# Delta rule kernel: unsigned bf16 matrix, first residual as two bf16 products, Wo loaded by quads, a PSUM bank of its own for the projection of v, a new static order

## The chip, the cores and the metric

One core of a Trainium2 chip. The metric is the device time of one launch in microseconds; lower is better.

## The reference, cut to what matters

The input x is 8 batches of 256 tokens of width 256. A modulated layer norm feeds a gated delta rule attention with 32 heads (keys of 48, values of 96), and a mixture of experts follows. Only the attention is touched:

```python
q = short_conv(h @ Wq, conv_q_w); k = short_conv(h @ Wk, conv_k_w)   # each followed by silu, 4 taps
v = short_conv(h @ Wv, conv_v_w)
q, k = l2norm(q), l2norm(k)
g = -exp(A_log) * softplus(h @ Wa + dt_bias); beta = sigmoid(h @ Wb)
def step(S, inp):                     # one token
    S = S * exp(g_t)
    delta = (v_t - k_t @ S) * beta_t
    S = S + outer(k_t, delta)
    return S, (q_t * scale) @ S
o = rmsnorm(o, gnorm_w) * silu(h @ Wg)
out = o.reshape(b, t, VD) @ Wo
```

## The kernel before, in words

`delta_rule` does the attention in 64 steps: 8 quads of four heads (the outer loop), each with 8 batches. A step treats 256 tokens as two chunks (c = 0, 1) of 128 tokens. Within a chunk the recurrence is a triangular system (I + A) w = r for each head, 128 x 128. `scores` and `decayed` make A (in `am`, plane 0, f32, with the query part in plane 1). An approximate inverse `tf` is built in bf16 from small blocks (`block`, `rows`, `base`, `expand`, `narrow1`, `narrow2`, `widen`, `merge1`, `merge2`). Then `w0` applies `tf` to the right side, and two rounds (REFINE = 2) refine it: `residual(c, r)` computes (I + A) w on TensorE with f32 operands and subtracts it from the right side on VectorE, giving `r16`; `delta(c, r)` adds `tf` times `r16` into the same bank CW, and ScalarE copies the sum to `w`. Chunk 0 yields the state S (`state_out`), which `ks` applies for chunk 1. `mean`, `gated`, `oT`, `wo`, `acc` finish the output.

The bf16 copy of A, `b16`, holds minus A. ScalarE makes it in `negate` directly from `am`; then GpSimd (in the helper `select`, called at the place `negate`) sets ones on the diagonals of `b16` and of `am` by two affine selects. ScalarE does not wait for GpSimd there.

The steps are a software pipeline of four stages. A turn runs one stage of four consecutive steps. `PLAN` gives a place to every piece; `TURN` sorts it by the place modulo 15 and every engine issues its own part of each piece in that order. Engines are in-order queues joined by semaphores, so a wait holds everything behind it on the same engine. There are 67 turns, of which 64 or so carry nearly all the pieces.

The eight PSUM banks are A0, A1, X0, X1, X2, CW, CX, CO; X2 is not used. `proj(n)` makes two of the six projected tiles (n = 0 and 1: q, k and part of v; n = 2: the rest of v) in banks A0, A1, A0. ScalarE scales them into `y`, VectorE adds three taps per tile (`taps(n, part)`), and ScalarE applies silu. `scores` also writes A0 and A1, so it waits in the first chunk until all taps have read their banks. GpSimd computes the squares, the decay diagonal (`gains`), the serial 8-row inverse (`base`, 15 small instructions), `root`, `keys_gain`, `keys_scale`, `block` and the output scale (`mean`). All of Wo (3072 KB) is loaded once, before the attention.

Of the kernel before, what the change touches and what calls it, by code (L numbers as in the profile page):

```python
# [63 lines left out]
PLAN = ((2.794, ("proj", 0)), (3.109, ("taps", 0, 0)), (3.26, ("taps", 0, 1)), (4.413, ("proj", 1)),  # L64
        (5.17, ("taps", 1, 0)), (5.463, ("silu", 0)), (5.907, ("taps", 1, 1)), (6.765, ("silu", 1)),
        (7.002, ("taps", 2, 0)), (7.474, ("gains",)), (7.927, ("proj", 2)), (8.48, ("norms",)),
        (9.634, ("taps", 2, 1)), (10.227, ("keys",)), (10.613, ("decays", 0)), (10.759, ("scores", 0)),
        (11.281, ("decayed", 0, 0)), (11.32, ("decayed", 0, 1)), (11.382, ("silu", 2)), (12.837, ("negate", 0)),
        (13.74, ("decays", 1)), (13.969, ("keys_scale",)), (14.149, ("decayed", 1, 0)), (14.381, ("scores", 1)),
        (14.667, ("decayed", 1, 1)), (14.991, ("negate", 1)), (16.191, ("gate", 0)), (17.05, ("gate", 1)),  # L70
        (17.595, ("root",)), (19.98, ("keys_gain",)), (20.599, ("values", 0)), (21.157, ("block",)),
        (21.281, ("round", 0)), (21.957, ("values", 1)), (24.173, ("rows",)), (26.886, ("base",)),
# [3 lines left out]
        (39.65, ("residual", 0, 0)), (40.95, ("delta", 0, 0)), (43.39, ("residual", 0, 1)),  # L76
        (43.577, ("delta", 0, 1)), (44.661, ("state_out",)), (45.952, ("ks",)), (46.296, ("w0", 1)),
        (46.395, ("mean", 0)), (47.508, ("gated", 0)), (47.55, ("residual", 1, 0)), (47.909, ("delta", 1, 0)),
        (49.242, ("oT", 0)), (49.665, ("residual", 1, 1)), (49.751, ("acc", 0)), (50.348, ("wo", 0)),
        (50.476, ("delta", 1, 1)), (50.81, ("out", 1)), (51.613, ("mean", 1)), (52.656, ("gated", 1)),  # L80
        (56.151, ("oT", 1)), (58.509, ("wo", 1)), (59.018, ("acc", 1)))
# [371 lines left out]
def delta_rule(nc, A, mem, scr):  # L453

    with ExitStack() as ctx:
# [169 lines left out]
        def _(pe):  # L625
            on = {n: nothing for n in PIECES}

            def merge1(st, l):
# [84 lines left out]
            def norms(st):  # L713
# [3 lines left out]
                for c in range(CH):  # L717
                    at = T + c * 2 * QH
                    for t in range(KTL):
                        last = pe.matmul(ps[:, A1, at:at + 2 * QH], sq[:, t, c * P:(c + 1) * P],  # L720
                                         const[:, C_HEAD + t * 2 * QH:C_HEAD + (t + 1) * 2 * QH],
                                         start=(t == 0), stop=(t == KTL - 1))
# [1000 lines left out]
```

## Time and profile before

| | |
|---|---|
| median of 3 runs | 2382.16 us (2377.2 to 2392.59) |
| the profiled execution | 2376.38 us; span 2374.4 us |
| TensorE busy | 2167.4 us, 91% |
| VectorE busy | 1801.3 us, 76% |
| GpSimd busy | 1420.4 us, 60% |
| ScalarE busy | 1196.1 us, 50% |
| the attention's turns | about 75 to 2035 us of the span |

The shares mix three phases: preparation (until 75 us), the attention, and the experts (from about 2035 us). The change is read from the middle phase, where the turns repeat. A matmul record's length contains the pipeline's latency, so the cost of a group to TensorE is the distance from its start to the next group's start.

### The profile page before, as it was taken

The numbers are of one execution on the slowest core, as the hardware profiler recorded it, in microseconds if no ns is written. First come the engines' busy times: TensorE is split into PE (matmuls) and PEld (weight loads), VectorE is DVE, ScalarE is ACT, GpSimd is POOL, SyncE is SP. The second block draws the span as 40 slices with busy tenths as digits, with TensorE's granted clock in tenths as the row PEclk, the third lists the DMA queues.
The fourth block names the chain that finished last, engine by engine and source line by source line (L and its number), as shares of the span: only waits on it lengthen the run. The fifth ranks groups of instructions, "written<-read, shape, count | busy, mean of one in ns | idle before, by whom it ended". The sixth has DMA issues, their size and how long they took to land. (4 is left out here: it accounts for less than half of the span.)

```text
span 2374.4 us, 50717 instructions
## 1 busy us (share of the span) xinstructions
PE 2167.4 (91%) x17776; PEld 1721.6 (73%) x17776; DVE 1801.3 (76%) x3955; ACT 1196.1 (50%) x3011; POOL 1420.4 (60%) x2176
## 2 busy tenths in 40 slices
PE   6489999999999999999999999999999998799997
PEld 2367777777777777777777777777777776455665
DVE  5678888888888888888888888888888885145544
ACT  4245555555555555555555555555555554222221
POOL 2567777777777777777777777777777774000000
PEclk9789999999999999999999999999999997799998
DMA  4211221112111211222112212212121110401100
GB/s 134 64 35 37 39 61 35 36 39 59 36 40 36 59 39 37 39 57 39 39 36 59 39 36 39 60 36 39 36 59 37 39 28 2 135 1 36 36 10 9
DMA packets 203838, 102.82 MB, mean 43 GB/s; under 512 B 97010, under 2 KB 185147, under 8 KB 203587
## 3 DMA queue, kind: packets, MB, share of 16 engines
q1 hardware_dynamic: 203266, 99.46, 18.5%
q8 instruction: 144, 2.36, 0.4%
q14 instruction: 108, 0.88, 0.1%
q10 hardware_dynamic: 320, 0.13, 0.0%
HBM read 69.69 MB, written 2.54 MB: 30 GB/s over the span
## 5 line engine op out<-in xcount | busy, mean ns | idle before, releaser
L911 DVE SCALAR_TENSOR_TENSOR dr_y<-dr_ps,cw,dr_y 128x255 f32<-128x255 f32 (+2 forms) x1152 | 476.1, 473 | 137.2 <-ACT dr_y L1044 137.2
L772 PE MATMUL dr_ps<-dr_w,dr_am 128*128 128x96 f32 x3072 | 438.0, 288 | 22.4 <-ACT dr_w L1096 22.4
L772 PEld LDWEIGHTS dr_ps<-dr_w,dr_am 128*128 128x128 f32 x3072 | 396.2, 198 | 57.5 <-ACT dr_w L1096 46.7
L1096 ACT COPY dr_w<-dr_ps 128x384 f32<-128x384 f32 x384 | 184.3, 480 | 292.0 <-PE dr_ps L772 292.0
L1044 ACT ACTIVATE dr_y<-dr_ps,cw 128x256 f32<-128x256 f32 x384 | 160.9, 470 | 138.8 <-PE dr_ps L704 137.2
L1194 POOL TENSOR_TENSOR dr_fo<-dr_vo,dr_nhalf 128x4 f32<-128x4 f32 x128 | 129.5, 1012 | 149.7 <-DVE dr_vo L982 145.0
L704 PE MATMUL dr_ps<-hT,wqk 128*128 128x256 f32 x768 | 195.5, 392 | 20.8 <-PEq L145 20.8
L955 DVE TENSOR_TENSOR dr_am<-dr_ps,dr_dec 128x512 f32<-128x512 f32 x256 | 164.9, 686 | 61.5 <-PE dr_ps L755 59.8
L1160 POOL TENSOR_TENSOR dr_dg<-const,dr_gam 128x512 f32<-128x512 f32 x128 | 130.3, 1039 | 126.5 <-DVE dr_gam L947 126.5
L838 PE MATMUL dr_ps<-wo,dr_oT 128*128 128x256 f32 x768 | 199.2, 397 | 1.1 <-ACT dr_oT L1132 1.0
L755 PE MATMUL dr_ps<-dr_qk 64*128 64x256 f32 x1024 | 161.2, 437 | 42.1 <-DVE dr_y L911 29.1
L733 PE MATMUL dr_ps<-wg,hT 128*128 128x384 f32 x512 | 194.8, 504 | 1.9 <-DVE dr_am L955 1.9
L704 PE MATMUL dr_ps<-hT,wv 128*128 128x256 f32 x768 | 186.9, 379 | 1.2 <-DVE dr_y L911 1.2
L1152 POOL TENSOR_TENSOR dr_sq<-dr_sy 128x256 f32<-128x256 f32 x128 | 75.7, 612 | 184.4 <-ACT dr_sy L1058 184.4
L1217 POOL TENSOR_TENSOR dr_xt<-dr_xb,dr_ab 128x56 f32<-128x56 f32 (+6 forms) x448 | 154.5, 345 | 39.4 <-ACT dr_ab L1092 0.2
L969 DVE TENSOR_TENSOR dr_r<-dr_rhs,dr_ps 128x384 bf16<-128x384 f32 x256 | 139.8, 546 | 49.5 <-PE dr_ps L772 49.5
L704 PEld LDWEIGHTS dr_ps<-hT,wqk 128*128 128x128 f32 x768 | 138.0, 193 | 36.0 <-issue 21.7
L923 DVE TENSOR_TENSOR_SCAN dr_dec<-dr_abc,dr_dg 128x512 f32<-128x512 f32 x128 | 160.8, 1256 | 0.1
L838 PEld LDWEIGHTS dr_ps<-wo,dr_oT 128*128 128x128 f32 x768 | 143.4, 201 | 16.5 <-ACT dr_oT L1132 1.5
L704 PEld LDWEIGHTS dr_ps<-hT,wv 128*128 128x128 f32 x768 | 140.9, 190 | 18.1 <-DVE dr_y L911 1.6
L755 PEld LDWEIGHTS dr_ps<-dr_qk 64*128 64x128 f32 x1024 | 98.2, 204 | 72.2 <-DVE dr_y L911 53.5
L1220 POOL TENSOR_TENSOR dr_xb<-dr_xb,dr_xt 128x56 f32<-128x56 f32 (+6 forms) x448 | 124.5, 278 | 35.1
(219 smaller groups left out, 4814.9 us busy)
## 6 DMA issues: line engine op xcount, KB each, us to landing
dr_abc<-scr_a SPq DMA_DIRECT2D x64, 512.0 KB, 5.4
dr_qk<-dr_sy SPq DMA_DIRECT2D x384, 48.0 KB, 2.0
dr_bcb<-scr_b SPq DMA_DIRECT2D x128, 64.0 KB, 4.8
dr_c<-dr_b SPq DMA_DIRECT2D x512, 4.0 KB, 1.8
dr_qk<-dr_sy SPq DMA_DIRECT2D x128, 32.0 KB, 1.9
ex_modb<-scr_mod SPq DMA_DIRECT2D x4, 1024.0 KB, 8.0
wv<-in_Wv SPq DMA_DIRECT2D x8, 384.0 KB, 3.5
wo<-in_Wo SPq DMA_DIRECT2D x1, 3072.0 KB, 12.0
```

The costliest lines, as they stand in the source:

```text
L704: last = pe.matmul(ps[:, BANK[n], j * T:(j + 1) * T], wt, hT[:, k, (it % B) * T:(it % B + 1) * T], start=(k == 0), stop=(k == KT - 1))
L733: last = pe.matmul(ps[:, (A0, A1)[c], 0:QV], hT[:, k, at:at + P], wg[:, k, :], start=(k == 0), stop=(k == KT - 1))
L755: last = pe.matmul(ps[:, (A0, A1)[side], a * 2 * P:(a + 1) * 2 * P], qk[lo:lo + 64, a, c, 0, :], qk[lo:lo + 64, a, c, :, :].rearrange("p n ...
L772: last = pe.matmul(ps[:, bank, h * DV:(h + 1) * DV], wt(h), x[:, h * DV:(h + 1) * DV], start=(start and h == 0), stop=(h == QH - 1), skip_ ...
L838: last = pe.matmul(ps[:, CO, 0:D], oT[:, t, :], wo[:, (it // B) * VT + t, :], start=(t == 0), stop=(t == VT - 1))
L911: v.scalar_tensor_tensor(y[:, slot, x:T], ps[:, BANK[n], off:off + T - x], cw[:, t, TAPS - 1 - x:TAPS - x], y[:, slot, x:T], ALU.mult, ALU ...
L923: v.tensor_tensor_scan(flat(dec[:, us, :]), flat(abc[:, m, c]), flat(dg[:, us, :]), 0.0, ALU.mult, ALU.add).then_inc(s["dec_ok"], 1)
L955: v.tensor_tensor(out, ps[:, (A0, A1)[side], :].rearrange("p (a n t) -> p a n t", a=PAIRS, n=2), bc(tri, 2, 2), ALU.mult).then_inc(s["am_o ...
L969: v.tensor_tensor(r16[:], rhs[:, m, c], ps[:, CX, 0:QV], ALU.subtract).then_inc(s["rs_ok"], 1)
L1044: act.activation(y[:, t % 4, :], ps[:, BANK[n], j * T:(j + 1) * T], ACT.Copy, scale=cw[:, t, TAPS - 1:TAPS]).then_inc(s["tap0"], 1)
L1096: act.copy(w[:, c, :], ps[:, CW, 0:QV]).then_inc(s["w_ok"], 1)
L1217: pool.tensor_tensor(xt[:, :, 0:left], bc(xb[:, :, j], 2, left), ab[:, j, :, j + 1:BASE], ALU.mult).then_inc(s["xs"], 1)
```

## The change: what it does

1. `b16` (minus A) becomes `a16` (plus A). The order of the two engines is turned: GpSimd first sets the diagonal of `am` (a piece of its own, `select`), then ScalarE casts it to `a16` (`negate`, now a plain copy waiting for GpSimd's `ia_ok`). The second affine select goes. The signs move into constants (masks) and into scales of ScalarE's copies.
2. The first residual of each chunk (r = 0) uses bf16: GpSimd makes `lo16` = am - a16 (piece `low`), and TensorE computes `a16` x `x16` plus `lo16` x `x16`, eight bf16 matmuls in place of four f32 ones. `x16` is minus the first solution, rounded to bf16 by ScalarE in `w0`; VectorE's `residual` adds instead of subtracting.
3. `delta(c, 0)` begins with one bf16 matmul of 384 columns by a negative identity `idn`, which restarts the sum in bank CW.
4. `proj(2)` writes the bank X2. `scores(0)` no longer waits for all taps but for those of `proj(0)`; `norms` is cut into two pieces, one per chunk.
5. Wo is loaded in parts of 384 KB, one per quad, into two alternating buffers.
6. `PLAN` has new places. On TensorE the order was: gate 0, narrow1 0, narrow2 0, w0 1, gate 1, narrow1 1, residual 1 0, narrow2 1, proj 0, delta 1 0, merge1 0, oT 0, proj 1, residual 1 1, wo 0, delta 1 1, merge2 0, values 0, out 1, merge1 1, values 1, proj 2, merge2 1, norms, w0 0, rows, residual 0 0, keys, scores 0, delta 0 0, oT 1, residual 0 1, wo 1, delta 0 1, scores 1, state_out, ks. It is now: ks, gate 0, gate 1, narrow1 0, w0 1, narrow2 0, residual 1 0, proj 0, narrow1 1, delta 1 0, oT 0, narrow2 1, proj 1, residual 1 1, merge1 0, wo 0, delta 1 1, values 0, merge2 0, out 1, merge1 1, values 1, proj 2, norms 0, merge2 1, norms 1, w0 0, rows, residual 0 0, keys, delta 0 0, oT 1, scores 0, residual 0 1, wo 1, delta 0 1, scores 1, state_out. On VectorE, `widen 1` now comes after `taps 0`, and `expand` after `ks`. On ScalarE `negate` 0 and 1 both follow the copies of `state_out` and precede that of `ks`; the gate's silus precede the copy of `w0 1`. On GpSimd, `select` 0 and 1 follow `base`, and `low`, `keys_gain`, the squares, `root`, `low`, `keys_scale`, `block` follow `mean 0`.

```diff
-PLAN = ((2.794, ("proj", 0)), (3.109, ("taps", 0, 0)), (3.26, ("taps", 0, 1)), (4.413, ("proj", 1)),
...
+PLAN = ((3.346, ("proj", 0)), (3.934, ("taps", 0, 0)), (4.167, ("taps", 0, 1)), (4.259, ("silu", 0)),
+        (5.544, ("proj", 1)), (7.832, ("taps", 1, 0)), (9.099, ("taps", 1, 1)), (9.319, ("silu", 1)),
+        (10.403, ("proj", 2)), (10.405, ("norms", 0)), (10.646, ("taps", 2, 0)), (10.696, ("gains",)),
+        (11.131, ("norms", 1)), (11.458, ("keys",)), (11.671, ("decays", 0)), (11.718, ("taps", 2, 1)),
+        (11.882, ("silu", 2)), (12.12, ("decayed", 0, 0)), (12.196, ("scores", 0)), (12.354, ("decayed", 0, 1)),
+        (13.634, ("decays", 1)), (13.825, ("scores", 1)), (13.831, ("select", 0)), (14.066, ("decayed", 1, 0)),
+        (14.166, ("select", 1)), (14.243, ("negate", 0)), (14.323, ("negate", 1)), (14.908, ("decayed", 1, 1)),
+        (15.869, ("gate", 0)), (16.014, ("gate", 1)), (16.781, ("low", 0)), (17.949, ("keys_gain",)),
+        (22.374, ("root",)), (22.752, ("values", 0)), (23.124, ("low", 1)), (23.185, ("keys_scale",)),
+        (23.656, ("block",)), (24.594, ("values", 1)), (25.169, ("round", 0)), (26.267, ("rows",)),
+        (27.391, ("base",)), (31.191, ("expand",)), (31.525, ("narrow1", 0)), (32.093, ("narrow2", 0)),
+        (32.93, ("widen", 0)), (33.497, ("narrow1", 1)), (34.109, ("narrow2", 1)), (34.998, ("widen", 1)),
+        (36.455, ("merge1", 0)), (38.215, ("merge2", 0)), (39.446, ("merge1", 1)), (40.621, ("merge2", 1)),
+        (41.188, ("w0", 0)), (41.444, ("residual", 0, 0)), (41.722, ("delta", 0, 0)), (42.317, ("residual", 0, 1)),
+        (42.66, ("delta", 0, 1)), (44.222, ("state_out",)), (45.358, ("mean", 0)), (45.459, ("ks",)),
+        (46.802, ("w0", 1)), (47.679, ("gated", 0)), (47.689, ("residual", 1, 0)), (48.602, ("delta", 1, 0)),
+        (48.824, ("oT", 0)), (51.162, ("residual", 1, 1)), (51.505, ("acc", 0)), (51.802, ("wo", 0)),
+        (51.903, ("delta", 1, 1)), (53.861, ("out", 1)), (55.155, ("mean", 1)), (56.485, ("gated", 1)),
+        (56.762, ("oT", 1)), (57.553, ("wo", 1)), (58.124, ("acc", 1)))
...
-        BANK = (A0, A1, A0)
+        BANK = (A0, A1, X2)
...
+            def out_weights(q):
+                wait(sp, s["wo_ps"], (q - 1) * B * CH)
+                sp.dma_start(wo[:, q % 2], A["Wo"][q * QV:(q + 1) * QV, :].rearrange("(t p) n -> p t n", p=P)
+                             ).then_inc(s["wo_ld"], 16)
...
                 if n == 2:
-                    pe.wait_ge(s["tap"], it * NT * 3 + 6)
+                    wait(pe, s["tap"], it * NT * 3)
...
-                        pe.wait_ge(*((s["tap"], (it + 1) * NT * 3), (s["kc_ok"], it + 1))[side])
+                        pe.wait_ge(*((s["tap"], it * NT * 3 + 6), (s["kc_ok"], it + 1))[side])
...
-                pe.wait_ge(s["ia_ok"], it * CH + c + 1)
-                heads(CX, lambda h: am[:, m, c * QH + h, 0, :], w[:, c, :], True).then_inc(s["res_ps"], 1)
+                if r == 0:
+                    pe.wait_ge(s["lo_ok"], it * CH + c + 1)
+                    heads(CX, lambda h: a16[:, m, c * QH + h, :], x16[:, c, :], True)
+                    heads(CX, lambda h: lo16[:, m, c * QH + h, :], x16[:, c, :], False).then_inc(s["res_ps"], 1)
+                else:
+                    pe.wait_ge(s["ia_ok"], it * CH + c + 1)
+                    heads(CX, lambda h: am[:, m, c * QH + h, 0, :], w[:, c, :], True).then_inc(s["res_ps"], 1)
...
+                if r == 0:
+                    pe.matmul(ps[:, CW, 0:QV], idn[:], x16[:, c, :], start=True, stop=False, skip_group_check=True)
...
-                act.wait_ge(s["am_ok"], it * 4 + 2 * c + 2)
-                act.activation(b16[:, m, c * QH:(c + 1) * QH, :], am[:, m, c * QH:(c + 1) * QH, 0, :], ACT.Copy,
-                               scale=-1.0).then_inc(s["b16_c"], 1)
+                act.wait_ge(s["ia_ok"], it * CH + c + 1)
+                act.copy(a16[:, m, c * QH:(c + 1) * QH, :], am[:, m, c * QH:(c + 1) * QH, 0, :]).then_inc(s["a16_ok"], 1)
...
-                copy_w(it, c, 0)
+                act.activation(x16[:, c, :], ps[:, CW, 0:QV], ACT.Copy, scale=-1.0).then_inc(s["w_ok"], 1)
...
-                wait(pool, s["b16_c"], it * CH + c + 1)
-                pool.affine_select(b16[:, m, us, :], b16[:, m, us, :], [[0, QH], [-1, P]], ALU.not_equal, 1.0, base=0,
-                                   channel_multiplier=1).then_inc(s["b16_ok"], 1)
+                pool.wait_ge(s["am_ok"], it * 4 + 2 * c + 2)
                 pool.affine_select(am[:, m, us, 0, :], am[:, m, us, 0, :], [[0, QH], [-1, P]], ALU.not_equal, 1.0, base=0,
                                    channel_multiplier=1).then_inc(s["ia_ok"], 1)
+
+            def low(st, c):
+                it, m = st
+                us = slice(c * QH, (c + 1) * QH)
+                pool.wait_ge(s["a16_ok"], it * CH + c + 1)
+                pool.tensor_tensor(lo16[:, m, us, :], am[:, m, us, 0, :], a16[:, m, us, :], ALU.subtract).then_inc(s["lo_ok"], 1)
```

## Rows read from the trace of the kernel before

**Rows 1.** Windows view, one turn: length; busy PE, PEld, DVE, ACT, POOL; granted clock; DMA.
```profile
840.00:869.20 29.20, 27.48 (x262) 23.12 (x264) 25.22 (x54) 17.03 (x44) 21.63 (x34) 1.00 0.19 39
```

**Rows 2.** Timeline of TensorE in that turn: start us, length us, line, result<-operands, records.
```profile
843.33 0.35 PE L677 MATMUL dr_ps<-dr_c32t,dr_b 128*128 128x32 bf16 x8
844.20 0.36 PE L688 MATMUL dr_ps<-dr_w,dr_tt 128*128 128x32 bf16 x8 [0.52 <-DVE dr_w L884]
844.50 0.33 PE L772 MATMUL dr_ps<-dr_rhs,dr_tf 128*128 128x96 bf16 x4
844.67 1.52 PE L733 MATMUL dr_ps<-wg,hT 128*128 128x384 f32 x4
...
846.23 1.11 PE L772 MATMUL dr_ps<-dr_w,dr_am 128*128 128x96 f32 x8
847.18 0.35 PE L688 MATMUL dr_ps<-dr_w,dr_tt 128*128 128x32 bf16 x8
847.38 1.97 PE L704 MATMUL dr_ps<-hT,wqk 128*128 128x256 f32 x8
...
861.53 1.13 PE L772 MATMUL dr_ps<-dr_w,dr_am 128*128 128x96 f32 x8 [0.16 <-ACT dr_w L1096]
862.50 0.38 PE L742 MATMUL dr_ps<-const,dr_qk 128*128 128x128 f32 x2
863.51 1.14 PE L755 MATMUL dr_ps<-dr_qk 64*128 64x256 f32 x8 [0.63 <-DVE dr_y L911]
...
872.53 0.35 PE L677 MATMUL dr_ps<-dr_c32t,dr_b 128*128 128x32 bf16 x8
```

**Rows 3.** Waits of TensorE, 500 to 1800 us (44 turns): total us, times, longest.
```profile
PE dr_ps L688 <- DVE dr_w L884: 22.9, 44, 0.5
```

**Rows 4.** Waits of VectorE in the same stretch, same columns.
```profile
DVE acc L994 <- PE dr_ps L838: 13.9, 43, 0.3
```

**Rows 5.** Timeline of VectorE in the same turn.
```profile
848.06 0.55 DVE L863 TENSOR_TENSOR dr_tn<-dr_c32t,bd 128x768 bf16<-128x768 bf16 x1
...
850.26 2.43 DVE L911 SCALAR_TENSOR_TENSOR dr_y<-dr_ps,cw,dr_y 128x255 f32<-128x255 f32 x6 [0.34 <-ACT dr_y L1044]
...
856.05 1.25 DVE L911 SCALAR_TENSOR_TENSOR dr_y<-dr_ps,cw,dr_y 128x254 f32<-128x254 f32 x3
...
867.13 1.27 DVE L923 TENSOR_TENSOR_SCAN dr_dec<-dr_abc,dr_dg 128x512 f32<-128x512 f32 x1
```

**Rows 6.** Timeline of ScalarE in the same turn.
```profile
841.94 0.62 ACT L1080 ACTIVATE dr_b<-dr_am 128x512 bf16<-128x512 f32 x1
...
857.11 0.58 ACT L1014 CAST dr_w<-dr_ps 64x512 bf16<-64x512 f32 x1
857.72 0.51 ACT L1086 CAST dr_rhs<-dr_rhs 128x384 bf16<-128x384 f32 x1
...
858.45 0.40 ACT L1060 ACTIVATE dr_vT<-dr_y 128x256 f32<-128x256 f32 x1
...
859.18 0.84 ACT L1044 ACTIVATE dr_y<-dr_ps,cw 128x256 f32<-128x256 f32 x2
```

**Rows 7.** Page, costliest groups: the copy of w.
```profile
L1096 ACT COPY dr_w<-dr_ps 128x384 f32<-128x384 f32 x384 | 184.3, 480 | 292.0 <-PE dr_ps L772 292.0
```

**Rows 8.** Timeline of GpSimd in the same turn.
```profile
861.91 2.04 POOL L1160 TENSOR_TENSOR dr_dg<-const,dr_gam 128x512 f32<-128x512 f32 x2 [1.90 <-DVE dr_gam L947]
863.89 1.20 POOL L1212 COPY dr_xb<-const 128x64 f32<-128x64 f32 x1
...
867.40 1.05 POOL L1217 TENSOR_TENSOR dr_xt<-dr_xb,dr_ab 128x32 f32<-128x32 f32 x1
868.53 0.25 POOL L1220 TENSOR_TENSOR dr_xb<-dr_xb,dr_xt 128x32 f32<-128x32 f32 x1
...
870.58 0.64 POOL L1180 TENSOR_SCALAR_AFFINE_SELECT dr_b<-dr_b 128x512 bf16<-128x512 bf16 x1
871.17 0.82 POOL L1182 TENSOR_SCALAR_AFFINE_SELECT dr_am<-dr_am 128x512 f32<-128x512 f32 x1
```

More of the change, by code:

```diff
@@ L62 @@
 ATANH = [1.0 / (2 * k + 1) for k in range(9)]
-PLAN = ((2.794, ("proj", 0)), (3.109, ("taps", 0, 0)), (3.26, ("taps", 0, 1)), (4.413, ("proj", 1)),
[L65 to L72, printed above, removed]
[3 rows of a table removed]
[L76 to L81, printed above, removed]
@@ L491, in delta_rule @@
         r16 = sb("r16", [P, QV], BF16)
+        x16 = sb("x16", [P, CH, QV], BF16)
+        lo16 = sb("lo16", [P, NB, U, P], BF16)
+        idn = sb("idn", [P, P], BF16)
         S = sb("S", [P, PAIRS, 2 * DV])
@@ L557, in delta_rule @@
         PIECES = ("merge1", "merge2", "w0", "delta", "residual", "ks", "out", "state_out", "mean", "gated", "oT", "wo",
-                  "acc", "rows", "block", "base", "expand", "narrow1", "narrow2", "widen", "proj", "silu", "taps", "gate", "norms", "gains", "root", "keys_gain", "decays", "keys", "keys_scale", "scores", "decayed", "negate",
+                  "acc", "rows", "block", "base", "expand", "narrow1", "narrow2", "widen", "proj", "silu", "taps", "gate", "norms", "gains", "root", "keys_gain", "decays", "keys", "keys_scale", "scores", "decayed", "select", "negate", "low",
                   "values", "round")
@@ L606, in blocks @@
                     rows = slice(2 * BASE * n, 2 * BASE * (n + 1))
-                    sp.dma_start(c16[rows], b16[rows, m, :, rows]).then_inc(s["c_st"], 16)
+                    sp.dma_start(c16[rows], a16[rows, m, :, rows]).then_inc(s["c_st"], 16)
             gate_weights(0)
@@ L635, in merge1 @@
                 for u in range(U):
-                    last = pe.matmul(ps[:, X0, u * 2 * HALF:(u + 1) * 2 * HALF], b16[:, m, u, :], cols[:, u],
+                    last = pe.matmul(ps[:, X0, u * 2 * HALF:(u + 1) * 2 * HALF], a16[:, m, u, :], cols[:, u],
                                      start=True, stop=True)
@@ L716, in norms @@
                 pe.wait_ge(s["sq_ok"], (it + 1) * KTL)
[L717 to L722, printed above, removed]
+                at = T + c * 2 * QH
+                for t in range(KTL):
+                    last = pe.matmul(ps[:, A1, at:at + 2 * QH], sq[:, t, c * P:(c + 1) * P],
+                                     const[:, C_HEAD + t * 2 * QH:C_HEAD + (t + 1) * 2 * QH],
+                                     start=(t == 0), stop=(t == KTL - 1))
                 last.then_inc(s["n_ps"], 1)
@@ L836, in wo_ @@
                 pe.wait_ge(s["oT_ok"], (it * CH + c + 1) * VT)
+                if c == 0:
+                    wait(pe, s["wo_ld"], it // B * 16)
                 for t in range(VT):
-                    last = pe.matmul(ps[:, CO, 0:D], oT[:, t, :], wo[:, (it // B) * VT + t, :],
+                    last = pe.matmul(ps[:, CO, 0:D], oT[:, t, :], wo[:, it // B % 2, t, :],
                                      start=(t == 0), stop=(t == VT - 1))
@@ L1221, in base @@
                     ins.then_inc(s["xb_ok"] if j == BASE - 2 else s["xs"], 1)
-            on.update(keys_scale=keys_scale, base=base, block=block, silu=squares, gains=gains, root=root, keys_gain=keys_gain, negate=select, mean=scale)
+            on.update(keys_scale=keys_scale, base=base, block=block, silu=squares, gains=gains, root=root, keys_gain=keys_gain, select=select, low=low, mean=scale)
             pool.memset(qk[:], 0.0).then_inc(s["set_ok"], 1)
```

48 lines of the change are left out of this document (26 added, 22 removed), and 3 rows, old and new, of the table PLAN.

## The prediction

> **What bounds the kernel now.** I read the totals first: TensorE is the busiest engine, but a share over three phases says little. So I went to the turns of the attention. Most of them repeat to a few hundredths of a microsecond. One instance, `narrow1 0` to `narrow1 0`, is 843.33 to 872.53, a period of 29.20 us [rows 2]. In a window of that length TensorE is busy 27.48 us and VectorE 25.22; GpSimd has 21.63 and ScalarE 17.03; the clock is 1.00, the upper level of 2.4 GHz [rows 1]. Two engines are nearly full, so the turn is set by TensorE's work plus those waits that VectorE, ScalarE and GpSimd cause it. The waits can be read as distances from start to start. `narrow1 0` holds the engine 0.87 us although its work is some 0.20 (`narrow2 1`, which does not wait, takes 847.18 to 847.38), because `narrow2 0` needs VectorE's masked copy: 0.52 us in each of 44 turns [rows 3]. `keys` takes 862.50 to 863.51, the last 0.63 of it waiting for the last tap [rows 2].
>
> **Part 1, the two bf16 products.** An f32 set of four head matmuls costs TensorE 0.97 us (861.53 to 862.50) or 0.95 (846.23 to 847.18); the bf16 set of the same shape 0.17 (844.50 to 844.67) [rows 2]. So `residual(c, 0)` falls from 0.96 to 2 x 0.17 = 0.34, twice a turn: 1.24 us less. `delta(c, 0)` gains one bf16 matmul of 384 columns, the same columns as the set: 0.17, twice, 0.34 more (bounds 0.10, without the three other weight loads, and 0.38, if an f32-like latency showed). Net 0.90 us less work per turn.
>
> The f32 set costs 5.6 times the bf16 set here [rows 2]. The Trainium skill (FP8 and Floating Point Precision, TensorE Precision Notes) says that true f32 makes four passes through the array; by that rule two bf16 products would cost half an f32 set, 0.48, and the net gain would be 0.62 us a turn. The rows' price is the one I use in the sum.
>
> **Part 2, waits on TensorE.** `w0 1` now stands between `narrow1 0` and `narrow2 0`, so the 0.52 us wait [rows 3] shrinks by 0.17 to about 0.35. The wait for the last tap in `scores(0)` goes, but `scores` had another lower bound just behind: `keys` ends at 862.88 and ScalarE's copy of about 0.4 has to follow, so that alone would free about 0.2 of the 0.63. The new order puts `delta 0 0` and `oT 1` there instead, which hides it, while `delta 0 0` itself may wait for VectorE. Together with the 0.90 us, TensorE could gain up to 1.5 us if nothing else were late. That is the floor, not the forecast.
>
> **Part 3, VectorE.** Its instructions are the same in number and form; only the order changes. In the order of after, `widen 1`, the taps of `proj 0` and `proj 1`, and what lies between form one dense block. Before, the block from `widen 1` to the last tap of `proj 1` ran from 848.06 to 857.30, 9.24 us, of which it stood 0.34 for ScalarE's copy and 0.32 (13.9/44) for `wo` [rows 4, 5]: 8.58 of work. The taps now come first, so that `widen 1` delays `residual 1 1`, `merge1 0` and all behind.
>
> **Part 4, GpSimd and ScalarE.** Out goes one affine select per chunk (0.64), in comes one subtraction of 128x512. The trace has no such instruction; `dg` of the same size takes 2.04 for two, 1.02 each, and the select 0.64 [rows 8]; between these I take 1.02, since it also has two operands. Net 0.4 x 2 = 0.8 us more (0 to 1.0), on an engine with 7.6 us idle, with its result needed only most of a turn later: nothing on the path. What is on the path is the new order of hands. Before, ScalarE cast A at 841.94 without asking GpSimd [rows 6]. Now the cast waits for `select`, and `select` stands behind `base`, which ends at 870.58, some 7 us after it starts [rows 8]. Behind the cast, on ScalarE, queue the rounding of chunk 1's right side (`ks`), the two gate silus and the copy `x16`; for `x16` TensorE's `residual 1 0` waits, and behind that `proj 0` with the next step's whole front.
>
> **The chain that sets the turn.** From the start of `proj 0` to the start of the next, with hops of about 0.05: `proj 0` 1.97 + 0.05 [rows 2]; ScalarE's two copies 0.84 + 0.03 [rows 6]; VectorE's block 8.58; then on ScalarE the last silu and the square (858.45 to 859.18) 0.73, the `merge1 1` copy (857.11 to 857.72) 0.61, `round` about 0.41 (its 0.51 less overlap), `proj 2` copies 0.84, hop 0.05: 2.64 [rows 6]; from their end (860.02) to the start of `dg` (861.91), which is three taps and `gains`: 1.89 [rows 6, 8]; `dg` 1.98 and `base` 6.69 (863.89 to 870.58) [rows 8]; two selects 1.25; the second cast 0.62 + 0.05; the rounding 0.51 + 0.05; two gate silus of 0.38 from start to start (an estimate from the 0.48 copy of the same size less 0.1 of overlap) 0.76; the `x16` copy 0.48 + 0.05 [rows 7]; `residual 1 0` 0.34. The sum is 2.02 + 0.87 + 8.58 + 2.64 + 1.89 + 8.67 + 1.25 + 0.67 + 0.56 + 1.63 = 28.78 us. The parallel leg without GpSimd, from `gains` over `decays`, taps, `decayed`, `scores 1`, `ks` and both gates to `proj 0`, I walked in the same way at about 28.3. The longer one sets the turn: 28.7 to 28.8 instead of 29.20. TensorE's 0.90 us then mostly turns into waiting.
>
> **Edits costed at nothing.** X2 for `proj 2`: its old wait (the first taps) is long satisfied before it starts. Wo by quads: seven transfers of 384 KB during the attention, issued behind those for the gate and ahead of `blocks`, whose data is wanted half a turn later; the wait in front of them asks for an output eight steps old. The smaller first load shortens nothing that waits. The split `norms`, `idn` and the new constants: the same records. If the cover of `blocks` were gone it would cost its own delay in eight turns only.
>
> **The sum.** 64 turns x 0.45 us = 29 us off the profiled 2376.4, so 2347. The median of the runs stands 5.8 above the profiled execution (2382.2), which would put it at 2353; part of that distance is scatter (the runs go from 2377.2 to 2392.6), and start and drain should gain a little too. I forecast 2350.
>
> **The rivals.**
> A: TensorE's saving gets through. If two or three links of the chain overlap better than I assume (the gate silus ahead of the rounding, a shorter `base`), the turn is 28.0 to 28.2, 1.1 us less x 64 = 70: 2312. For it: the net work is 0.9 less. Against it: VectorE's dense block.
> B: slower. The cast behind `select` behind `base` is late. Every microsecond that `base` or `select` is late reaches `proj 0` undiminished; from 0.45 us on nothing is left of the gain. The price: a small `base` instruction took 1.05 us instead of 0.25 while VectorE's scan ran from 867.13 to 868.40; the POOL instruction ended with it [rows 5, 8], and one select took 0.82 instead of 0.64 [rows 8]. Two more such hits, 0.8 each less 0.4, give +0.4 to +1.2 a turn: 2376 + 0.6 x 64 = 2414 for the middle.
> The Trainium skill (SBUF — State Buffer, Who interferes with whom) says that a VectorE instruction with two SBUF inputs and a GpSimd one that reads SBUF lock each other out for the whole instruction; the trace agrees (1.05 us against 0.25). By that rule `low`, two reads more on GpSimd, adds places where VectorE's `widen` is held.
> C: no change: VectorE binds, and the turn stays within 0.2 us of 29.2; the bf16 saving comes off TensorE's waiting alone: 2376 to 2390 for the median.
>
> **How the numbers follow.** About 1% (24 us) is what a measurement of this kernel can tell from no change. My forecast, 2350 with 2330 to 2370, gets 0.41; A 0.22, B 0.17, C 0.20. The forecast lies four fifths below 2358, so faster by over 1%: 0.33 + 0.22 = 0.55; within: 0.08 + 0.20 = 0.28; slower: 0.17. The range takes most of A (from 2300) and all of C, and stops short of B's middle: 2300 to 2396.
>
> **What would show it.** Right: a turn of 28.6 to 28.9 us; the bf16 residual with 0.34 to the next start; ScalarE's casts to `a16` right behind the second `select`, and TensorE waiting for `x16` or for VectorE's `r16`. TensorE's busy time down by 0.9 us a turn and its idle time up by half of it. A shows as casts that come well before the rounding needs ScalarE; B as ScalarE standing for `am` ahead of `ks`. Wrong it would be if a wait that I don't see (the order of VectorE behind `gains`, the `qk` transfers before `keys`) is longest.

## The result

The changed kernel takes 2432.5 us (median of 4 runs, 2424.8 to 2436.4) against 2387.1 for the kernel before on the same chip: ratio 1.0203, 95% interval 1.0166 to 1.0240. I had forecast 2350 and a range of 2300 to 2396. It is slower by 2%, outside the range, and on the other side of the forecast.

The head of its page and the clock line of its slices:

```profile
span 2433.5 us, 50973 instructions
...
PE 2211.1 (91%) x17904; PEld 1710.6 (70%) x17904; DVE 1826.4 (75%) x3955; ACT 1228.0 (50%) x3012; POOL 1478.3 (61%) x2176
...
PEclk8689999999999999999999998999999998799998
```

Every engine's share is about the same as before, and TensorE's granted clock has more slices below 9. The turns say more. The starts of `keys`, one per step, run from 92.3 to 2019.4 us; in the kernel before from 92.0 to 1960.8. That is 30.59 against 29.66 us per turn, and 63 times the difference is 58 of the 59 us between the profiled executions (2435.4 and 2376.4). So the loss lies in the repeating turns alone. (The medians are 45 us apart, not 59: the kernel before varies from 2377 to 2393 us, and its profiled execution is a fast one.)

```profile
L751 PE MATMUL dr_ps<-const,dr_qk x128: 272/421/477, 92.3 to 2019.4; 128*128 128x128 f32 x128
```

The next windows are of the changed kernel: 1600 us of turns, and one turn without a clock drop. In the kernel before, the first of these windows has a granted clock of 0.98, here it has 0.93.

```profile
160.00:1760.00 1600.00, 1502.82 (x13690) 1221.08 (x13688) 1331.44 (x2821) 919.17 (x2298) 1171.20 (x1728) 0.93 0.19 43
```
```profile
900.74:930.63 29.89, 27.39 (x263) 22.11 (x262) 25.68 (x55) 17.66 (x44) 22.68 (x34) 1.00 0.15 38
```

TensorE is busy 27.39 of 29.89 us, where it was 27.48 of 29.20 [rows 1]. So two things went wrong: the undisturbed turn is 0.69 us longer, and the clock is at its lower level (1.2 GHz, shown as 0.5) more often: 302 us of the 63 turns against 114. Only three of the 63 turns have no such stretch. The clock's part is 30.59 - 29.89 = 0.70 us a turn, against 29.66 - 29.20 = 0.46 before (the first turns of both kernels, at low clock, included). Over 63 turns: 44 us by the longer turn, 15 by the clock.

**TensorE in that turn**, in the form of [rows 2]:

```profile
900.74 0.35 PE L687 MATMUL dr_ps<-dr_c32t,dr_b 128*128 128x32 bf16 x8
...
911.75 0.81 PE L729 MATMUL dr_ps<-const,dr_sq 128*128 128x8 f32 x6 [0.34 <-ACT dr_sq L1083]
...
914.14 0.34 PE L781 MATMUL dr_ps<-dr_rhs,dr_tf 128*128 128x96 bf16 x4 [0.68 <-ACT dr_tf L1045]
...
915.06 0.34 PE L781 MATMUL dr_ps<-dr_x,dr_a 128*128 128x96 bf16 x4 [0.17 <-ACT dr_x L1120]
915.24 0.33 PE L781 MATMUL dr_ps<-dr_x,dr_lo 128*128 128x96 bf16 x4
915.41 0.40 PE L751 MATMUL dr_ps<-const,dr_qk 128*128 128x128 f32 x2
916.22 0.34 PE L810 MATMUL dr_ps<-dr_x,dr_idn 128*128 128x384 bf16 x1 [0.41 <-DVE dr_r L988]
...
927.36 0.35 PE L687 MATMUL dr_ps<-dr_c32t,dr_b 128*128 128x32 bf16 x8
927.56 0.33 PE L781 MATMUL dr_ps<-dr_rhs,dr_tf 128*128 128x96 bf16 x4
928.23 0.37 PE L698 MATMUL dr_ps<-dr_w,dr_tt 128*128 128x32 bf16 x8 [0.34 <-DVE dr_w L902]
...
928.84 1.96 PE L714 MATMUL dr_ps<-hT,wqk 128*128 128x256 f32 x8
930.63 0.35 PE L687 MATMUL dr_ps<-dr_c32t,dr_b 128*128 128x32 bf16 x8
```

The parts that I had priced behave as priced. The bf16 residual takes 915.06 to 915.41, 0.35 for both products (0.34 forecast); the identity matmul 0.18; `narrow2 0` waits 0.34 (0.35 forecast); `scores` has no wait for a tap. What is new is a wait of 0.68 before `w0 0` (914.14) and one of 0.41 before `delta 0 0`; the one before `norms` grows from 0.19 to 0.34. All three are behind VectorE and ScalarE. One sign that I had named did not show: TensorE's busy time fell by 0.09 us, not 0.9.

**VectorE**, in the form of [rows 5]:

```profile
904.16 0.55 DVE L881 TENSOR_TENSOR dr_tn<-dr_c32t,bd 128x768 bf16<-128x768 bf16 x1
...
907.96 0.56 DVE L980 TENSOR_TENSOR dr_rhs<-dr_ps,dr_nrm 128x384 f32<-128x384 f32 x1 [0.78 <-POOL dr_nrm L1187]
908.43 2.42 DVE L929 SCALAR_TENSOR_TENSOR dr_y<-dr_ps,cw,dr_y 128x255 f32<-128x255 f32 x6
...
916.64 1.99 DVE L941 TENSOR_TENSOR_SCAN dr_dec<-dr_abc,dr_dg 128x512 f32<-128x512 f32 x1
```

The block from `widen 1` now has a hole of 0.78 us before `values 0` (907.96), for `nrm` from GpSimd. And the first scan takes 1.99 us; in the turn of before the first took 1.22 (the scan in [rows 5], 1.27, is that turn's second).

**GpSimd**, in the form of [rows 8]:

```profile
904.53 1.73 POOL L1172 TENSOR_TENSOR dr_sq<-dr_sy 128x256 f32<-128x256 f32 x2 [3.73 <-ACT dr_sy L1077]
906.22 1.63 POOL L1187 TENSOR_TENSOR dr_nrm<-dr_kk,dr_half 128x8 f32<-128x8 f32 x1
...
915.51 2.04 POOL L1180 TENSOR_TENSOR dr_dg<-const,dr_gam 128x512 f32<-128x512 f32 x2 [1.48 <-DVE dr_gam L965]
```

`root` (L1187) stands behind the squares, which wait for silu 0 and then take 1.73 us; it ends at 907.85, and VectorE goes on at 907.96. In the order of before `root` stood right behind `mean 0`, ahead of `keys_gain` and the squares. The long scan starts at 916.64, while `dg` runs on GpSimd until 917.55, and ends 1.08 us after that, where a scan alone takes 1.22: nearly all of it ran only when `dg` was done. In the order of before, the scan came behind `taps 2 1` and so behind `dg`, which ended at 863.95 there [rows 8]. `root` and the first scan in the turn of before:

```profile
847.05 1.64 POOL L1167 TENSOR_TENSOR dr_nrm<-dr_kk,dr_half 128x8 f32<-128x8 f32 x1
```
```profile
863.84 1.22 DVE L923 TENSOR_TENSOR_SCAN dr_dec<-dr_abc,dr_dg 128x512 f32<-128x512 f32 x1
```

The Trainium skill (SBUF — State Buffer, Who interferes with whom) has this as an exclusive lock for a VectorE instruction with two SBUF inputs against a GpSimd one that reads SBUF; the trace agrees, with 1.99 against 1.22 us once the two are apart (e3_both, below).

### The profile page after: what moved, and what is told of

Read it like the earlier page. It is cut to its first block and busy times, and to the rows that moved or that the text cites. A ratio compares the mean times of both kernels' runs of the same rounds, so it can differ in the third digit from the quotient of the medians.

```text
span 2433.5 us, 50973 instructions
## 1 busy us (share of the span) xinstructions
PE 2211.1 (91%) x17904; PEld 1710.6 (70%) x17904; DVE 1826.4 (75%) x3955; ACT 1228.0 (50%) x3012; POOL 1478.3 (61%) x2176
## 5 line engine op out<-in xcount | busy, mean ns | idle before, releaser
L781 PEld LDWEIGHTS dr_ps<-dr_w,dr_am 128*128 128x128 f32 x2048 | 277.2, 205 | 39.6 <-issue 28.1
L781 PE MATMUL dr_ps<-dr_w,dr_am 128*128 128x96 f32 x2048 | 298.1, 292 | 0.0
L1172 POOL TENSOR_TENSOR dr_sq<-dr_sy 128x256 f32<-128x256 f32 x128 | 109.7, 876 | 251.1 <-ACT dr_sy L1077 251.1
L1115 ACT COPY dr_w<-dr_ps 128x384 f32<-128x384 f32 x256 | 122.7, 479 | 269.2 <-PE dr_ps L781 269.2
L941 DVE TENSOR_TENSOR_SCAN dr_dec<-dr_abc,dr_dg 128x512 f32<-128x512 f32 x128 | 197.9, 1546 | 2.9 <-POOL dr_dg L1180 2.9
L764 PE MATMUL dr_ps<-dr_qk 64*128 64x256 f32 x1024 | 173.1, 463 | 11.4 <-DVE dr_am L973 8.1
L742 PE MATMUL dr_ps<-wg,hT 128*128 128x384 f32 x512 | 180.4, 497 | 1.9 <-DVE dr_am L973 1.9
L1244 POOL TENSOR_TENSOR dr_xb<-dr_xb,dr_xt 128x56 f32<-128x56 f32 (+6 forms) x448 | 139.1, 311 | 35.1
L1241 POOL TENSOR_TENSOR dr_xt<-dr_xb,dr_ab 128x56 f32<-128x56 f32 (+6 forms) x448 | 126.3, 282 | 39.3
L1207 POOL TENSOR_TENSOR dr_lo<-dr_am,dr_a 128x512 bf16<-128x512 f32 x128 | 148.4, 1160 | 0.0
```

Of the source, the lines that this page charges most:

```text
L742: last = pe.matmul(ps[:, (A0, A1)[c], 0:QV], hT[:, k, at:at + P], wg[:, k, :], start=(k == 0), stop=(k == KT - 1))
L764: last = pe.matmul(ps[:, (A0, A1)[side], a * 2 * P:(a + 1) * 2 * P], qk[lo:lo + 64, a, c, 0, :], qk[lo:lo + 64, a, c, :, :].rearrange("p n ...
L781: last = pe.matmul(ps[:, bank, h * DV:(h + 1) * DV], wt(h), x[:, h * DV:(h + 1) * DV], start=(start and h == 0), stop=(h == QH - 1), skip_ ...
L941: v.tensor_tensor_scan(flat(dec[:, us, :]), flat(abc[:, m, c]), flat(dg[:, us, :]), 0.0, ALU.mult, ALU.add).then_inc(s["dec_ok"], 1)
L1207: pool.tensor_tensor(lo16[:, m, us, :], am[:, m, us, 0, :], a16[:, m, us, :], ALU.subtract).then_inc(s["lo_ok"], 1)
L1244: ins = pool.tensor_tensor(xb[:, :, j + 1:BASE], xb[:, :, j + 1:BASE], xt[:, :, 0:left], ALU.add)
```

## The experiments

"Clean turn" is the distance between the starts of `keys` in two turns between which the clock stays up (the middle value of all such pairs); "mean turn" is the distance from the first start to the last, divided by 63. All kernels were timed against the kernel before, in four groups of one chip each: the changed one; e1 to e4; e5, e6, e8 and e9; e7 and e10 to e12. The kernel before took 2387.1, 2380.3, 2376.2 and 2374.5 us there, so between rows of different groups the ratio says more than the microseconds.

| kernel | clean turn | mean turn | clock, 160 to 1760 us | median us | ratio to before (95%) |
|---|---|---|---|---|---|
| before | 29.20 | 29.66 | 0.98 | 2374.5 to 2387.1 | 1 |
| changed | 29.89 | 30.59 | 0.93 | 2432.5 | 1.020 (1.017 to 1.024) |
| e1_root_early | 29.04 | 29.14 | 0.99 | 2340.0 | 0.982 (0.980 to 0.985) |
| e2_scan_late | none | 30.60 | 0.92 | 2430.0 | 1.019 (1.015 to 1.023) |
| e3_both | 28.41 | 28.71 | 0.98 | 2316.2 | 0.972 (0.968 to 0.975) |
| e4_old_order | none (33.9 in most) | 33.97 | 0.93 | 2644.5 | 1.110 (1.106 to 1.113) |
| e5_fill | 29.89 | 29.93 | 1.00 | 2388.7 | 1.006 (1.004 to 1.007) |
| e6_scan_fill | 29.18 | 29.20 | 1.00 | 2343.3 | 0.986 (0.982 to 0.989) |
| e8_old_order_cast_late | 30.0 | 30.17 | 0.97 | 2406.3 | 1.012 (1.008 to 1.016) |
| e9_round_merge_early | 28.75 | 29.25 | 0.97 | 2348.9 | 0.988 (0.984 to 0.992) |
| e10_both_fill | 28.41 | 28.42 | 1.00 | 2293.6 | 0.965 (0.961 to 0.968) |
| e7_f32_residual | 29.58 | 29.89 | 0.98 | 2390.0 | 1.006 (1.003 to 1.009) |
| e11_before_fill | 29.21 | 29.19 | 1.00 | 2343.6 | 0.985 (0.981 to 0.989) |
| e12_both_old_bank | 28.93 | 29.42 | 0.98 | 2354.3 | 0.990 (0.986 to 0.994) |

**e1_root_early, e2_scan_late, e3_both: the two waits.** My theory after the two traces: VectorE's path sets the turn, and two waits on it had no price in my sum. The places that move:

```diff
-        (22.374, ("root",))
+        (16.5, ("root",))            # e1, e3: behind mean 0, ahead of low
-        (11.718, ("taps", 2, 1))
+        (11.66, ("taps", 2, 1))      # e2, e3: ahead of decays 0
```

> The changed kernel with one place altered: GpSimd's root (nrm) runs right behind mean 0, ahead of low, keys_gain and the squares, as it did before the change. Theory R (two unpriced waits on VectorE's path set the turn, one of them root behind the squares, 0.78 us in front of values 0): that wait goes, the clean turn falls from 29.89 to 29.1 us, the run from 2432 to about 2385 us. Theory B (ScalarE's cast behind select behind base sets the turn): nothing of that moves, the turn stays at 29.9, 2430 us. Theory C (TensorE's half-clock stretches are the loss): the clean turn may fall, but the mean turn stays over 30.4 and the time over 2420.

> The changed kernel with one swap on VectorE: taps(2, 1) ahead of decays(0), so that the scan starts after GpSimd has finished dg. Theory R: the scan falls from 1.99 to about 1.25 us and the clean turn from 29.89 to about 29.15, the time to 2388 us. Theory B: scan shorter, turn unchanged, 2430 us. Theory C: mean turn over 30.4 still.

> Both edits: root early and the scan behind taps(2, 1). Theory R: both sit in one chain, so they add: clean turn 28.4 us (29.89 - 0.78 - 0.74), time 2340 us. Theory B: 29.9 and 2430. If one of the two merely covered the other, the turn is that of the better single edit, 29.1, 2385 us.

e1 has a clean turn of 29.04 (29.1 expected) and e3 of 28.41 (28.4 expected). VectorE and GpSimd in e3_both, and its waits of TensorE:

```profile
1004.66 0.56 DVE L980 TENSOR_TENSOR dr_rhs<-dr_ps,dr_nrm 128x384 f32<-128x384 f32 x1
...
1014.43 1.22 DVE L941 TENSOR_TENSOR_SCAN dr_dec<-dr_abc,dr_dg 128x512 f32<-128x512 f32 x1
```
```profile
1024.16 1.64 POOL L1187 TENSOR_TENSOR dr_nrm<-dr_kk,dr_half 128x8 f32<-128x8 f32 x1
```
```profile
1010.84 0.34 PE L781 MATMUL dr_ps<-dr_rhs,dr_tf 128*128 128x96 bf16 x4 [0.42 <-ACT dr_tf L1045]
```

`values 0` follows `acc` without a gap (1004.66), the scan takes 1.22, and `root` runs at 1024.16, before `low`. The wait before `w0 0` falls from 0.68 to 0.42. The two edits together give 1.48 us of clean turn. And e1 alone, one place in a table of sorted keys, turns 2% slower into 1.8% faster.

Which chain sets the turn is shown by what ScalarE waits for between `state_out` and `x16`. These lines are of the waits over 500 to 1800 us (total, times, longest), of e1 and of e6_scan_fill, the reverse case: the scan moved and `root` left, with filler that is explained below.

```profile
ACT dr_gs L1089 <- PE dr_ps L742: 26.3, 45, 0.6
```
```profile
ACT dr_a L1107 <- POOL dr_am L1208: 33.1, 45, 0.8
```

While the scan meets `dg` (e1, 45 times; the changed kernel, 43 times, beside 20 shorter waits for GpSimd, 5.7 us in all), ScalarE waits for TensorE's second gate: the leg over VectorE and TensorE is the longer one. With the scan moved (e6, e10: 45 times; e3: 36, the gate 10 times), ScalarE's cast waits for GpSimd's `select` in place of it: now the chain over `dg`, `base`, `select` and the cast is the longer. In e3 its links on ScalarE follow each other without a gap:

```profile
1021.51 1.21 ACT L1099 CAST dr_a<-dr_am 128x512 bf16<-128x512 f32 x2 [0.73 <-POOL dr_am L1200]
1022.62 0.51 ACT L1145 CAST dr_rhs<-dr_rhs 128x384 bf16<-128x384 f32 x1
1023.03 1.00 ACT L1089 ACTIVATE dr_gs<-dr_ps 128x384 f32<-128x384 f32 x2
1023.94 0.48 ACT L1120 ACTIVATE dr_x<-dr_ps 128x384 bf16<-128x384 f32 x1
```

The time of e1 came out 45 us below the expected, because the clock recovered as well (0.99; 83 us at the lower level against 302), and that of e3 24 us below. e2 missed its expectation altogether: 2430 us, mean turn 30.60, though its scan is short. It has no clean turn at all. Its turns alternate between 29.6 and 31.9 us, those of the changed kernel between 29.7 and 31.7; two together are 61.4 us in both. Theory C, the clock, was right for this run: whatever the scan gave back went into the half-clock stretches. In both traces the half-clock stretches come at the same distance: they begin 30.7 us apart, one after the other, from 944.0 to 1097.6 us in the changed kernel and from 942.6 to 1096.2 in e2. The turns keep step with them, and so the mean is the same. That called for the next two.

**e5_fill, e6_scan_fill: the clock alone.** TensorE gets bf16 matmuls that nobody reads where it waits anyway.

```diff
+            def fill(n):
+                for _ in range(n):
+                    pe.matmul(ps[:, CW, QV:QV + P], id16[:], id16[:], start=True, stop=True, skip_group_check=True)
...
+                if c == 0:
+                    fill(6)                    # in norms, ahead of its wait for sq_ok
...
+                if c == 0:
+                    fill(10)                   # in w0, ahead of its wait for tt_ok
```

> The changed kernel, with 6 idle bf16 matmuls (128 columns, into unread columns of bank CW) before norms 0 and 10 before w0 0, where TensorE waits 0.34 and 0.68 us anyway. Theory D (the half-clock stretches of the changed kernel come from TensorE's waits in that part of the turn): their total falls from 302 us towards the 80 to 115 us of the kernel before, the mean turn from 30.58 to about 29.95, the time to about 2395. Rival (they come from something else: the mix of matmuls, or the total load): they stay, and the time is 2430 or more.

> The filler of e5_fill together with taps(2, 1) ahead of decays(0), the edit that alone brought nothing (2430 us). If the half-clock stretches had eaten its gain (mean turn 30.63 in both), the clean turn shows now, 29.15 us, and the time is about 2350 to 2360. If root's wait covers the scan's (one chain hides the other), the turn stays at 29.9 and the time at that of e5_fill.

The first fence is the changed kernel where the clock falls, the second e5_fill at the same place of a turn, the third e5's window over the turns:

```profile
941.65 0.81 PE L729 MATMUL dr_ps<-const,dr_sq 128*128 128x8 f32 x6 [0.35 <-ACT dr_sq L1083]
...
944.04 0.50 PE L781 MATMUL dr_ps<-dr_rhs,dr_tf 128*128 128x96 bf16 x4 [0.68 <-ACT dr_tf L1045]
```
```profile
1016.57 0.50 PE L783 MATMUL dr_ps<-id 128*128 128x128 bf16 x6
1016.99 0.83 PE L731 MATMUL dr_ps<-const,dr_sq 128*128 128x8 f32 x6
...
1018.58 0.72 PE L783 MATMUL dr_ps<-id 128*128 128x128 bf16 x10
1019.46 0.34 PE L787 MATMUL dr_ps<-dr_rhs,dr_tf 128*128 128x96 bf16 x4 [0.17 <-ACT dr_tf L1053]
```
```profile
160.00:1760.00 1600.00, 1509.90 (x14876) 1232.51 (x14875) 1368.00 (x2888) 943.36 (x2354) 1206.31 (x1762) 1.00 0.20 45
```

In the changed kernel the bf16 set at 944.04 lasts 0.50 us and not 0.33: the clock has fallen, right after the waits of 0.35 and 0.68. In e5 the two waits are filled (16 matmuls, 0.42 and 0.72 us), the turn is the same 29.89, and the clock over the 1600 us is 1.00. The mean turn falls by 0.66, the time by 44 us (1.4% by the ratios). So the clock falls because TensorE stands in this part of the turn, and with the waits filled it costs nothing. The filler also makes TensorE busier as a whole; that its busy time over the turn is what counts is unlikely, since e8 (below) has less of it, 26.91 of 30.00 us, and a clock of 0.97, but filler in another part of the turn was not tried. e6 then shows the scan's edit undisturbed: 29.18 (29.15 expected), 0.71 less than 29.89. This gain had been there all the time in e2, hidden by the clock. The time, 2343 us, is a little under the expected 2350 to 2360.

The Trainium skill (TensorE: Matmul & The Clock Gate, HAM oscillation — how this bites in real kernels) says that waits which come back in every iteration can put TensorE back to half clock in every iteration, and shows it with waits for DMA of 3 to 5 us. Here single waits of 0.3 to 0.7 us, in a part of the turn with several of them, do it.

**e4_old_order, e8_old_order_cast_late: the new arithmetic in the old order.** e4 is the changed kernel with the places of before (`norms`, `select`, `low` put in beside `norms`, `negate`, `root`); e8 moves one piece.

```diff
-        (12.836, ("select", 0)), (12.837, ("negate", 0))     # e4
+        (12.836, ("select", 0)), (14.67, ("negate", 0))      # e8: on ScalarE behind state_out
```

> The changed kernel (unsigned a16, first residual as two bf16 products, Wo by quads, bank X2) with the places of the kernel before; norms, select and low are inserted beside norms, negate and root. If the new order is what costs, this is faster than the kernel before by part of the 0.9 us of saved TensorE work: clean turn 28.6 to 29.0, time 2345 to 2375 us. If the new arithmetic costs (two more GpSimd instructions, the cast behind select), the turn is over 29.2 and the time over 2390 us.

> The changed kernel in the order of before as in e4_old_order, but with negate 0 on ScalarE behind the copies of state_out in place of ahead of delta 0 1. Theory B's mechanism (ScalarE held by the cast that waits for select behind base, 3.54 us on TensorE each turn) explains the 2644 us if this one drops by some 3.5 us a turn, to about 2400 or below: clean turn 28.8 to 29.6, time 2355 to 2410. If the rest of the new arithmetic is dear in the old order, it stays over 2450.

ScalarE and TensorE in e4:

```profile
1012.80 0.62 ACT L1098 CAST dr_a<-dr_am 128x512 bf16<-128x512 f32 x1 [4.83 <-POOL dr_am L1199]
1013.33 0.47 ACT L1114 COPY dr_w<-dr_ps 128x384 f32<-128x384 f32 x1
```
```profile
1013.85 0.91 PE L829 MATMUL dr_ps<-dr_w,dr_kg 128*64 128x96 f32 x8 [3.54 <-ACT dr_w L1114]
```

The cast (L1098) waits 4.83 us for the select behind `base`; the copy of `w` stands behind it, and TensorE's `state_out` waits 3.54 us for that. This is one form of rival B, real and large, but only where the cast stands ahead of `delta 0 1`. I had expected 28.6 to 29.0 of this run, and its own alternative, over 29.2, came true by far. With the cast moved (e8) 238 us come back. The time is within the expected 2355 to 2410, the clean turn of 30.0 above the expected 28.8 to 29.6. It is still 1.2% slower than before: in the old order `narrow2` waits 1.2 us a turn (51.2 us over 43) for VectorE. So the new arithmetic loses in the old places, as I had put its pieces there (other insertions were not tried), and gains in the new order once two details are mended (e3).

**e7_f32_residual and e12_both_old_bank: parts undone in the good order.** e7 also drops the identity matmul and lets `w0` copy to `w`; e12 also takes back the two waits that go with the bank.

```diff
-                if r == 0:
-                    pe.wait_ge(s["lo_ok"], it * CH + c + 1)
-                    heads(CX, lambda h: a16[:, m, c * QH + h, :], x16[:, c, :], True)
-                    heads(CX, lambda h: lo16[:, m, c * QH + h, :], x16[:, c, :], False).then_inc(s["res_ps"], 1)
...
-        BANK = (A0, A1, X2)
+        BANK = (A0, A1, A0)
```

> e3_both with the first residual done again as four f32 matmuls on w, without the identity matmul; low is still computed on GpSimd and unused. It gives TensorE back the 0.90 us of work that the change took off. If the good order makes TensorE's work count, the clean turn goes from 28.41 to 29.0 to 29.3 and the time to 2350 to 2375; if the saving was covered by waits (TensorE not the bound), it stays within 0.3 us: 2316 to 2335.

> e3_both with proj 2 back in bank A0 and with it the old waits (scores 0 for all taps of its step). The last tap ends 0.6 us after scores 0 starts in e3_both, so scores 0 is late by up to 0.6: clean turn 28.6 to 29.0, time 2325 to 2350. If other work covers that, 28.4 and 2316.

e7: the clean turn is 29.58, 1.17 more than e3_both; that is above the 0.90 of work. A part of the rest is found in its trace: from `residual 1 1` to `merge1 0` TensorE takes 1.13 us, 0.86 in e3. I take it that the first residual lies on the path with its latency too, so that VectorE's results come later; that was not tested. Both turn and time, 2390, lie above the expected 29.0 to 29.3 and 2350 to 2375. ScalarE waits for the second gate again (44 turns), so it is the leg over TensorE that became longer. e12: 28.93, 0.52 more, with a wait for the tap of 0.61 in `scores 0`, as expected for the turn; the time, 2354, is just above the expected 2325 to 2350, with 131 us at the lower clock against 80 in e3:

```profile
1007.28 1.13 PE L764 MATMUL dr_ps<-dr_qk 64*128 64x256 f32 x8 [0.61 <-DVE dr_y L929]
```

**e9_round_merge_early: a further move that failed.**

```diff
-        (25.169, ("round", 0))
+        (24.2, ("round", 0))
...
-        (39.446, ("merge1", 1))
+        (39.1, ("merge1", 1))
```

> e3_both with two more moves on ScalarE: round 0 and the copy of merge1 1 ahead of silu 1, so that they fill its 0.9 us wait for the taps in place of standing between silu 1 and the copies of proj 2. In the chain as I have it both leave it (0.41 and 0.61): clean turn 28.41 to 27.5 to 27.9, time 2270 to 2295. If VectorE or TensorE is the bound there, nothing: 2316.

I had read the 0.94 us in which ScalarE waits for the taps in the changed kernel and took it for granted in e3. But it was the shadow of `root`: with `root` early it is gone. ScalarE in e3_both, then in e9:

```profile
1006.67 0.49 ACT L1130 ACTIVATE dr_sqo<-dr_ps 128x384 f32<-128x384 f32 x1 [0.48 <-PE dr_ps L781]
1007.27 0.42 ACT L1077 ACTIVATE dr_sy<-dr_y 128x256 f32<-128x256 f32 x1
```
```profile
963.33 0.49 ACT L1130 ACTIVATE dr_sqo<-dr_ps 128x384 f32<-128x384 f32 x1 [0.48 <-PE dr_ps L781]
963.85 0.59 ACT L1033 ACTIVATE dr_w<-dr_ps 64x512 bf16<-64x512 f32 x1
964.46 0.51 ACT L1104 CAST dr_rhs<-dr_rhs 128x384 bf16<-128x384 f32 x1
964.88 0.41 ACT L1077 ACTIVATE dr_sy<-dr_y 128x256 f32<-128x256 f32 x1
```

In e3 silu 1 starts 0.60 us after the squares of `out 1`; there is no room. With the two copies in between it starts 1.55 after, the square for `norms` is late, and TensorE waits 0.43 there. The wait of 0.42 before `w0 0` goes for it, but from the start of `proj 2` to that of `keys` TensorE now takes 5.33 us in a clean turn, 5.06 in e3. The turn rises to 28.75, the time to 2349 where 2270 to 2295 was expected.

**e10_both_fill and e11_before_fill: filler on the good order and on the kernel before.** The filler of e5, with 6 ahead of `w0 0` and 5 ahead of `delta 0 0` in e10, and 3 ahead of `norms` and 10 ahead of `scores 0` in e11.

> e3_both with idle bf16 matmuls where TensorE waits: 6 before w0 0 (wait 0.42 us), 5 before delta 0 0 (0.41). The clean turn stays at 28.4; the half-clock total (80 us in e3_both, of which some 30 fall into the first two turns) falls to about 35, the mean turn from 28.73 to 28.45, the time from 2316 to about 2300. If the filler delays the work behind it, the clean turn rises to 28.5 or more and nothing is won.

> The kernel before with idle bf16 matmuls ahead of its two waits in that part of the turn (3 before norms, 10 before scores 0). If waits there bring on half-clock stretches in the kernel before too, its total of 114 us in the turns falls towards 40, the mean turn from 29.70 to 29.25, the time from 2380 to about 2350; the clean turn stays 29.20. Rival: the filler brings nothing or delays: 2380 to 2400.

Both came out as expected. e10, 2293.6 us, is the fastest: 3.5% below the kernel before. e11 is the kernel before with 13 useless matmuls per turn: the same clean turn of 29.2, 1.5% less time. So, filler against filler, the mended change is worth 2.1% (2293.6 against 2343.6 us). The window of e10:

```profile
160.00:1760.00 1600.00, 1547.19 (x15366) 1290.83 (x15367) 1415.43 (x3040) 976.70 (x2478) 1279.42 (x1856) 1.00 0.21 47
```

## Why the prediction was wrong

- **What bounds the kernel**: right. The turn is set by TensorE's work plus the waits that the other engines cause it, and those waits grew by more than the work fell.
- **Part 1** (0.90 us of TensorE work): right in size by the starts (0.35 for the two products, 0.18 for the identity), and where the other waits are gone it counts in full and more (1.17, e7). My statement that it mostly turns into waiting was wrong for the good order.
- **Part 2**: right in the main. `narrow2 0` waits 0.34; the freed `scores 0` is worth 0.52 in this order (e12), where I had read about 0.2 from the old one.
- **Part 3**, VectorE: here is the first of the two terms that failed. I took the block at its 8.58 us of work and did not look at what it receives: `root` had been moved behind the squares, so `nrm` comes 0.78 us late in the middle of the block. From the first of the taps (901.82) to the last of `proj 1` (910.85) VectorE takes 9.03 us, of which 8.25 are work.
- **The parallel leg, "about 28.3"**: here is the second. The scan that meets `dg` on GpSimd had no price in it, and it costs 0.71 us of turn (e6 against e5). My last sentence on what would make the forecast wrong named VectorE's order behind `gains`, which is where this scan stands, but the term was not in the sum; I had the lock in the text, and applied it only to `base` and `low`. With it the leg became the longer of the two: 29.04 in e1, where `root` no longer waits. Less the scan's 0.7 that is about 28.3 (an estimate), so the rest of the walk was good.
- **The chain over GpSimd and the cast, 28.78**: right in kind, and too long by 0.37. It sets the turn of e3 (28.41), and 0.33 of the difference is VectorE's block, 8.25 us of work for the forecast 8.58. With `root`'s wait in it, it is 29.18 (e6). In the changed kernel it was the shorter one: there ScalarE stood 0.58 us for the second gate.
- **Together**: `root`'s wait is in the part that both chains share, the scan's in one. The changed kernel's turn is 28.41 + 0.78 + 0.70 = 29.89 us in place of the forecast 28.75. Alone, the two edits give 0.85 (e1) and 0.71 (e6), 0.08 more than both together in e3; where these 0.08 go was not traced. The two terms that I put at nothing are larger than the whole gain of 0.45 that I had forecast.
- **Part 4 and rival B**: the direction was B's, the mechanism was not. Its price was also summed wrongly: the middle of 0.4 and 1.2 is 0.8, not 0.6, and gives 2427 us. That it would have come near the measured 2432.5 is luck, since the cause was another. The rest of part 4 is near: GpSimd's busy time rose by 1.05 us a turn (0.8 forecast). B's wait exists (3.54 us in e4, 0.73 in e3, the better kernel), but in this turn of the changed kernel the cast runs at 924.84 to 926.05 without waiting, and `x16` waits for the second gate's matmuls:

```profile
924.84 1.21 ACT L1099 CAST dr_a<-dr_am 128x512 bf16<-128x512 f32 x2
926.07 0.51 ACT L1145 CAST dr_rhs<-dr_rhs 128x384 bf16<-128x384 f32 x1
...
927.56 0.49 ACT L1089 ACTIVATE dr_gs<-dr_ps 128x384 f32<-128x384 f32 x1 [0.58 <-PE dr_ps L742]
927.95 0.48 ACT L1120 ACTIVATE dr_x<-dr_ps 128x384 bf16<-128x384 f32 x1
```

- **Edits at nothing** (Wo by quads, the wait of `proj 2`, the constants): between 500 and 1800 us the trace has no wait of TensorE for Wo, and two for the `qk` transfers, 0.7 us in all. They were not undone one by one.
- **Missing altogether**: the clock. I took it as given. It cost 0.24 us a turn more than before, 15 of the 59 us, and hid the whole of e2's gain. It is not the main error: with filler the changed kernel is still 0.6% slower than the kernel before (e5).

## What to carry to other kernels

When a static order is laid out anew, list for each piece on the full engines what it receives from the less loaded ones, and check where each of those producers now stands in its own queue: a 1.6 us instruction on an engine with 7 us idle cost nearly 4% of the kernel (2432 against 2340 us), the clock's part included. Price a VectorE instruction like this scan and a GpSimd one like `dg` as one queue where they meet (1.99 us against 1.22 here). When two chains share a part, ask of each wait which of them it is in: one in the shared part counts in full, one in a single chain only from where that chain is the longer. And compare kernels by the clean turn and by the granted clock separately: filling TensorE's short recurring waits with work that nobody reads was worth 0.7% to 1.5% here by the ratios (e10 against e3, e5 against the changed kernel, e11), and it shows whether an edit that "brings nothing" has only been eaten by the clock.

## What I had not expected of the hardware

Recurring waits of TensorE of at most 0.7 us, in a turn in which it is busy 92% of the time, were enough to bring the granted clock from 1.00 to 0.93 over 1600 us. Sixteen idle matmuls of 128 columns per turn brought it to 1.00. With the drops, the turns of two kernels whose undisturbed turns differ by 0.71 us took the same mean time (30.59 and 30.60 us), with the half-clock stretches 30.7 us apart in both. Why they come at that distance stays open; only the filler was tried.
